# A new order of the work ahead of the attention: softmax before the weight copies, four banks for the values, the norm in two halves of six tiles, and two weight jobs on GpSimd

## What is computed

```python
tokens = conv(x, conv_w, stride 4) + conv_b            # (4, 256, 192)
q, k, v = tokens @ {q,k,v}_w.T + {q,k,v}_b             # 96 wide
img = softmax(q @ k.T / sqrt(96)) @ v @ proj_w.T + proj_b
h = concat(img, txt)                                   # (4, 384, 192)
x_norm = ln(h) ; qkv = x_norm @ Wqkv + bqkv
hidden = silu(x @ Wb1)                                 # x is itself a normed h
h = h + linear_attention(qkv, hidden) @ Wproj + bproj
h = h + experts(ln(h); router_w, w1, w2, top 2 of 8)
```

## Time and profile before

| | |
|---|---|
| runs | 320.44, 320.45, 321.77 us; median 320.45 |
| profiled execution | 316.02 us |
| its span, first to last instruction | 314.3 us |
| busy: PE, DVE, ACT, GpSimd | 76%, 68%, 56%, 37% |
| mean granted clock of PE | 0.872 of 2.4 GHz |
| PE of the chain that ended last | 43% (DVE 24%, ACT 13%, issue 8%, DMA 5%) |

### The profile page before, as it was taken

The page is one execution under the profiler, slowest core; times in us unless marked ns, Lnnn a source line. Parts: engine busy times, 40 slices in busy tenths (PEclk is TensorE's granted clock), DMA queues, the critical chain, the costliest instruction groups (busy, mean ns, idle before and its releaser), DMA issues.

```text
span 314.3 us, 7309 instructions
## 1 busy us (share of the span) xinstructions
PE 239.6 (76%) x2381; PEld 173.0 (55%) x2382; DVE 214.7 (68%) x661; ACT 175.5 (56%) x410; POOL 117.0 (37%) x151
## 2 busy tenths in 40 slices
PE   3876965795767379787969897489999999999400
PEld 3265554353444257466648675357777677777200
DVE  2184986789986648688886799636566566556565
ACT  1347153378788798998891354045655456555100
POOL 5000014154542123223221031455767677773301
PEclk9999977579997597999995589589999999999955
DMA  6991005000000002130001021021122111110085
GB/s 178 313 238 40 3 0 168 34 0 3 1 0 3 0 2 60 45 102 3 4 0 41 0 77 38 25 63 53 62 63 72 45 61 54 41 38 32 7 265 186
DMA packets 13390, 19.01 MB, mean 60 GB/s; under 512 B 3451, under 2 KB 11138, under 8 KB 12850
## 3 DMA queue, kind: packets, MB, share of 16 engines
q1 hardware_dynamic: 10018, 13.90, 14.6%
q0 software_dynamic: 3024, 4.73, 5.1%
q10 hardware_dynamic: 320, 0.01, 0.1%
HBM read 14.69 MB, written 5.41 MB: 64 GB/s over the span
## 4 chain that ended last, share of the span: by engine, by line
PE 43%; DVE 24%; ACT 13%; issue 8%; DMA 5%; SPq 4%; POOL 1%; DVEq 0%; ACTq 0%; POOLq 0%
PE bank L983 4%; PE bank L996 3%; PE bank L998 3%; PE bank L997 3%; DMA qk<-in_w1b 3%; PE bank L900 2%; PE bank L968 2%; DVE third_place L1421 2%; PE bank L972 2%; PE bank L971 2%; PE bank L970 2%; PE bank L969 2%; PE bank L954 2%; DMA v<-y_rows 2%; DVE at_half L1471 2%
## 5 line engine op out<-in xcount | busy, mean ns | idle before, releaser
L1234 ACT ACTIVATE qk<-bank 128x512 f32<-128x512 f32 x31 | 18.5, 597 | 48.6 <-PE bank L972 48.6
L564 POOL DMA_INDIRECT qk<-x_rows,tok_row x32 | 34.7, 1085 | 20.8 <-DVE tok_row L1746 9.4
L569 POOL DMA_INDIRECT y_rows<-qk,dst_row x31 | 31.3, 1010 | 20.6 <-DVE qk L1786 13.7
L996 PE MATMUL bank<-wx,qk 128*128 x124 | 30.5, 246 | 0.7 <-DVE qk L1780 0.5
L997 PE MATMUL bank<-wx,qk 128*128 x124 | 30.5, 246 | 0.0
L998 PE MATMUL bank<-wx,qk 128*128 x124 | 30.5, 246 | 0.0
L1780 DVE COPY qk<-bank 128x512 f16<-128x512 f16 x31 | 13.1, 424 | 24.9 <-PE bank L983 24.3
L1471 DVE SCALAR_TENSOR_TENSOR at_half<-bank,at_half 128x384 f16<-128x384 f32 x48 | 25.1, 549 | 5.0 <-ACT at_half L1149 4.8
L1774 DVE TENSOR_TENSOR qk<-qk 128x512 f16<-128x512 f32 x31 | 21.4, 692 | 10.2 <-ACT qk L1235 10.2
L1149 ACT ACTIVATE at_half<-bank 128x384 f16<-128x384 f32 x48 | 21.3, 511 | 3.6 <-PE bank L800 3.6
L983 PEld LDWEIGHTS bank<-ident,qk 128*128 128x128 f16 x248 | 16.2, 98 | 8.8 <-DVE qk L1774 2.2
(11 more groups left out here) (323 smaller groups left out, 711.2 us busy)
## 6 DMA issues: line engine op xcount, KB each, us to landing
early<-in_w SPq DMA_DIRECT2D x4, 768.0 KB, 4.4
qk<-in_w1a SPq DMA_DIRECT2D x2, 1024.0 KB, 6.0
qk<-in_w1b SPq DMA_DIRECT2D x4, 512.0 KB, 10.3
x_rows<-xr SPq DMA_DIRECT2D x4, 288.0 KB, 2.3
v<-y_rows SPq DMA_DIRECT2D x4, 288.0 KB, 4.9
qk<-y_rows SPq DMA_DIRECT2D x4, 288.0 KB, 5.2
out<-hr SPq DMA_DIRECT2D x4, 288.0 KB, 2.9
at_half<-in_wq SPq DMA_DIRECT2D x1, 704.0 KB
```

The costliest lines, as they stand in the source:

```text
L564: pool.indirect_dma_start(xg[:, i % 4, :], None, x2_dram, bass.IndirectOffsetOnAxis(ap=tok_row[:, i:i + 1], axis=0), bounds_check=NTOK - 1 ...
L569: pool.indirect_dma_start(y_dram, bass.IndirectOffsetOnAxis(ap=dst_row[:, i:i + 1], axis=0), ye[:, i % 4, :], None, bounds_check=2 * NTOK ...
L996: pe.matmul(o_, actT[:, k, 0, c], w[:, W2H + d:W2H + d + D], start=(m == 0), stop=False)
```

## The change

On PE: eight products of a matrix of ones with itself ahead of the first wait; the second half of `g` goes to bank 4; values go to banks 5, 6, 7, 4 and wait for no copy of values; the bias products move ahead of the transpositions of images 0 and 1 (and wait for all four value copies, whose banks they reuse); scores run one step ahead of `himg`; the small products for the output projection move between images 2 and 3; 50 instead of 60 fillers ahead of the slot products, none in place of 20 ahead of the experts.

On ACT: softmax 0 and 1 and the values come before any weight copy; it takes over the copies of the transposed probabilities; weight jobs 0 to 3 are copied behind the values, softmax 2, softmax 3 and image 2. Jobs 0 and 1 are copied with scale 1, since GpSimd scaled them in place.

On GpSimd: it scales jobs 0 and 1 in place when they land, and forms their low halves, job 0's before and job 1's behind the low half of the projection weights, both ahead of `x_low(0)`.

On DVE: no low halves of jobs 0 and 1 and no copies of probabilities; text moments follow the first two maxima; job 2's low half comes behind the maxima of all images, job 3's between `normalize(1)` and `x_t(0)`; the first norm takes six tiles; moments of images 2 and 3 and the second norm (six tiles) are a chain whose steps are put between the instructions of the loop's first rounds (`go_on`), to be finished before tile 6 is normalized.

The counts of `s_w_low` are lowered by two where they are waited for (SP, GpSimd, PE, ACT), and PE and ACT also wait for `s_w_pool_low` at 4. The diff, cut to its core:

```diff
+            def scaled(n):
+
+                w, _high, _low = staged(n)
+                pool.wait_ge(s_w_loaded[n], 16)
+                pool.tensor_scalar(w, w, WS, None, ALU.mult).then_inc(s_w_scaled, 1)
+
+            def pool_low(n):
+
+                pool.wait_ge(s_w_high, n + 1)
+                for half in range(2):
+                    w, high, low = staged(n, half)
+                    pool.tensor_tensor(low, w, high, ALU.subtract).then_inc(s_w_pool_low, 1)
+
+            scaled(0)
+            scaled(1)
+            pool_low(0)
             pool.wait_ge(s_wqhigh_ready, 2)
             pool.tensor_tensor(bias_half[:, 1, :], bq, bias_half[:, 0, :], ALU.subtract).then_inc(s_biaslow_ready, 1)
             pool.tensor_tensor(w_half[:, 1, 0, :], wq[:, 0, :], w_half[:, 0, 0, :], ALU.subtract).then_inc(s_wqlow_ready, 1)
             pool.tensor_tensor(w_half[0:D - P, 1, 1, :], wq[0:D - P, 1, :], w_half[0:D - P, 0, 1, :], ALU.subtract).then_inc(s_wqlow_ready, 1)
 
+
+            pool_low(1)
...
+            pe.wait_ge(s_ones_ready, 1)
+            for _ in range(8):
+                pe.matmul(bank[3][:, 0:P], ones[:], ones[:], start=True, stop=True)
...
-            for i in range(2):
-                if i:
-                    pe.wait_ge(s_g_ready, i)
-                pe.matmul(bank[7][0:NP1, :], mt[:], xp1[:, i * 512:(i + 1) * 512], start=True, stop=True).then_inc(s_g_mm, 1)
+            for i, bk in enumerate((7, 4)):
+                pe.matmul(bank[bk][0:NP1, :], mt[:], xp1[:, i * 512:(i + 1) * 512], start=True, stop=True).then_inc(s_g_mm, 1)
...
-                    pe.wait_ge(s_vp_ready, i - 1)
+                    pe.wait_ge(s_g_ready, i - 1)
...
-                    mm = pe.matmul(bank[5 + i % 2][:, n * D:(n + 1) * D], xp1[:, m0:m0 + P], wv, start=True, stop=True)
+                    mm = pe.matmul(bank[VALUES_AT[i]][:, n * D:(n + 1) * D], xp1[:, m0:m0 + P], wv, start=True, stop=True)
...
-                if b == 0:
-                    pe.wait_ge(s_vp_ready, B)
+                pe.wait_ge(s_vp_ready, b + 1)
...
             scores(0)
             scores(1)
             for i in range(B):
                 values(i)
+            bias_products()
             prob_t(0)
             prob_t(1)
...
-            mm.then_inc(s_mnb_mm, 1)
+            scores(2)
             himg(0)
-            scores(2)
+            scores(3)
             himg(1)
-            scores(3)
             prob_t(2)
+            projection_t()
+            himg(2)
             prob_t(3)
-            himg(2)
+            router_products()
             himg(3)
...
-            keep_busy(60)
+            keep_busy(50)
...
-            keep_busy(20)
...
-                act.activation(high, w, ACT.Copy, scale=WS).then_inc(s_w_high, 1)
+                if n < 2:
+                    act.wait_ge(s_w_scaled, n + 1)
+                else:
+                    act.wait_ge(s_w_loaded[n], 16 * (2 if jobs[n][0] == "w1b" else 1))
+                act.activation(high, w, ACT.Copy, scale=1.0 if n < 2 else WS).then_inc(s_w_high, 1)
 
...
+            def prob_t(b):
+                act.wait_ge(s_pT_mm, b + 1)
+                if b >= 2:
+                    act.wait_ge(s_himg_mm, b - 1)
+                act.activation(probT[:, b % 2, :, :].rearrange("p a n -> p (a n)"), bank[2 + b % 2][:, :], ACT.Copy).then_inc(s_pT_ready, 1)
...
             softmax(0)
+            values(0)
+            values(1)
             softmax(1)
-            weights_high(3)
-            for b in range(B):
-                himg(b)
-                if b + 2 < B:
-                    softmax(b + 2)
-                if b == 1:
-
-                    act.wait_ge(s_wq_ready, 5)
-                    act.activation(w_half[:, 0, :, :], wq, ACT.Copy).then_inc(s_wqhigh_ready, 1)
-                    act.wait_ge(s_bq_ready, 1)
-                    act.activation(bias_half[:, 0, :], bq, ACT.Copy).then_inc(s_wqhigh_ready, 1)
-
+            values(2)
+            values(3)
+            weights_high(0)
+            prob_t(0)
+            prob_t(1)
+            himg(0)
+            softmax(2)
+            weights_high(1)
+            himg(1)
+            softmax(3)
+            weights_high(2)
+            act.wait_ge(s_wq_ready, 5)
+            act.activation(w_half[:, 0, :, :], wq, ACT.Copy).then_inc(s_wqhigh_ready, 1)
+            act.wait_ge(s_bq_ready, 1)
+            act.activation(bias_half[:, 0, :], bq, ACT.Copy).then_inc(s_wqhigh_ready, 1)
+            prob_t(2)
...
+            himg(2)
+            weights_high(3)
+            prob_t(3)
...
+            himg(3)
...
-            weights_low(0)
             negmax(0)
             negmax(1)
+            dve.wait_ge(s_txt_loaded, 16 * B)
+            for b in range(B):
+                moments(b * CT + IT, h[:, b * CT + IT, :])
...
+            row_sums(0)
+            row_sums(1)
             biases()
             negmax(2)
             weight_scales()
             negmax(3)
-            prob_t(2)
-            image_moments(0)
-            image_moments(1)
-            prob_t(3)
-            image_moments(2)
-            two_norms(0, T - CT)
+            row_sums(2)
+            row_sums(3)
+            weights_low(2)
+            finish(image_moments(0))
+            finish(image_moments(1))
+            finish(two_norms(0, 2 * CT))
...
+            def last_rows_norm():
+                yield from image_moments(2)
+                yield from image_moments(3)
+                yield from two_norms(2 * CT, T)
+
             normalize(0)
             normalize(1)
+            weights_low(3)
             x_t(0)
-
-            for n in range(IT):
-                dve.wait_ge(s_himg_ready, (B - 1) * IT + n + 1)
-                moments((B - 1) * CT + n, h[:, (B - 1) * CT + n, :])
-            two_norms(T - CT, T)
+            rows = last_rows_norm()
...
+                if t + 2 == 2 * CT:
+                    finish(rows)
+                go_on(rows)
                 if t + 2 < T:
                     normalize(t + 2)
 
                 dve.wait_ge(s_exp_ready, t + 1)
-                link(dve.tensor_scalar(eb[:, t % 2, :], eb[:, t % 2, :], FS, None, ALU.min))
+                n_min = after(dve.tensor_scalar(eb[:, t % 2, :], eb[:, t % 2, :], FS, None, ALU.min))
+                go_on(rows)
+                dve.wait_ge(s_step, n_min)
...
+                go_on(rows)
...
+                go_on(rows)
+                go_on(rows)
                 if t:
                     queries_low(t - 1)
+                go_on(rows)
+                go_on(rows)
```

More of the change, by code:

```diff
@@ L1317, in weights_low, with moments @@
                     ins.then_inc(s_w_low, 1)
+            def moments(t, src):
+                link(dve.bn_stats(stat[:, t, :], src))
+                link(dve.bn_aggr(mv[:, t, :], stat[:, t, :]))
             def negmax(b):
@@ L1374, in two_norms @@
                 a, r = nwt[:, 0, 0:2 * n], nwt[:, 1, 0:2 * n]
-                link(dve.tensor_scalar(a[:, 0:n], mv[:, t0:t1, 1], EPS, None, ALU.add))
-                link(dve.scalar_tensor_tensor(out=a[:, n:2 * n], in0=a[:, 0:n], scalar=EPS, in1=mv[:, t0:t1, 1], op0=ALU.mult, op1=ALU.add))
-                for _ in rsqrt_steps(r, a, 2 * n):
-                    pass
+                k = after(dve.tensor_scalar(a[:, 0:n], mv[:, t0:t1, 1], EPS, None, ALU.add))
+                yield
+                dve.wait_ge(s_step, k)
+                k = after(dve.scalar_tensor_tensor(out=a[:, n:2 * n], in0=a[:, 0:n], scalar=EPS, in1=mv[:, t0:t1, 1], op0=ALU.mult, op1=ALU.add))
+                yield
+                dve.wait_ge(s_step, k)
+                yield from rsqrt_steps(r, a, 2 * n)
                 dve.tensor_copy(r12[:, t0:t1], r[:, n:2 * n])
@@ L1392, in prob_t @@
-                dve.tensor_copy(probT[:, b % 2, :, :].rearrange("p a n -> p (a n)"), bank[2 + b % 2][:, :]).then_inc(s_pT_ready, 1)
             def image_moments(b):
-                for n in range(IT):
-                    dve.wait_ge(s_himg_ready, b * IT + n + 1)
-                    moments(b * CT + n, h[:, b * CT + n, :])
-            dve.wait_ge(s_txt_loaded, 16 * B)
-            for b in range(B):
-                moments(b * CT + IT, h[:, b * CT + IT, :])
-            weights_low(1)
-            weights_low(2, (0,))
@@ L1404, in _ @@
-            prob_t(0)
-            prob_t(1)
-            weights_low(2, (1,))
-            weights_low(3)
+                for t in range(b * CT, b * CT + IT):
+                    dve.wait_ge(s_himg_ready, b * IT + t % CT + 1)
+                    k = after(dve.bn_stats(stat[:, t, :], h[:, t, :]))
+                    yield
+                    dve.wait_ge(s_step, k)
+                    k = after(dve.bn_aggr(mv[:, t, :], stat[:, t, :]))
+                    yield
+                    dve.wait_ge(s_step, k)
@@ L1408, in _, with go_on, finish, together @@
+            def go_on(chain):
+                next(chain, None)
+            def finish(chain):
+                for _ in chain:
+                    pass
```

(13 more changed lines are left out.)

101 lines of the change are left out of this document (49 added, 52 removed).

## The result

The changed kernel takes 321.23 us (median of 20 runs, 319.62 to 327.35), the kernel before 320.24 on the same chip (20 runs, 316.55 to 322.37). The ratio counts only executions within 1.5% of the fastest of their kernel (12 of the 20 before, 19 of the 20 after), and by it the changed kernel takes 1.0128 of the time before, with an interval of 1.0103 to 1.0153. The size is less sure than that interval looks: the means of the executions counted, 318.65 and 321.27 us, differ by 0.8%, and the medians of all 20 by 1.0 us, 0.3%. So it is **slower, by 0.3 to 1.3%**, 1 to 4 us; measured again (last but one of the experiments) it was 1.019 by the ratio and 1.3% by the medians. The profiled execution took 320.58 us around a span of 318.8, against 316.02 and 314.3.

The account below looks back on a forecast made before the run. It took chains of waits over the first 75 us and the seam before the expert loop as the bound; +1.9 at tile 5 and -1.0 at the seam gave +0.9, so 321.3 us, range 315.0 to 325.0.

Parts of the forecast that it names:

- Set-up, "I take 0" for the clock: PE's start: whether eight products of ones raise the clock, 0 to -1.9 us on set-up products; 0 taken.
- Bias products, 28.9: PE's bias products ahead of the transposes: start 24.0, last 4.9 us, end 28.9 (-6.4); wholly at 1.2 GHz, 30.2.
- Copy 2 ends at 39.3, the high halves at 41.2: ACT's weight copy 2, then projection weights' and bias's high halves: done at 41.2 instead of 45.6, -4.4 us.
- N: Start of the first normalized tile on DVE, ahead of the expert loop: 53.2 us, forecast not to move.
- rival B: PE stays at 1.2 GHz through bias products and transposes; DVE 1.3 to 3 us later: 322.6 to 324.5; chance 0.25.
- A: The forecast itself: -1.5 to +2.5 us as the clock at set-up and the seam fall, 319.0 to 323.0; chance 0.42.
- Each step lets one whole GpSimd instruction pass: DVE's six-tile norm beside GpSimd's queue: four instructions end during it, the fourth at 50.3; thirteen steps left, 2.8 us.
- Rival C: Small norm steps slip past GpSimd; first normalized tile at 48 to 51, total 315.0 us; chance 0.20.
- After N: First loop rounds: tile 0 2 us later, tile 1 -0.5, moments and norm steps in gaps; +1.9 at tile 5.
- Seam, -1.0: Before the expert loop, without 20 fillers: transposes start earlier, first expert products at low clock; 0 to -3, taken -1.0 us.
- Rival E: Nothing moves: bias products' wait for parameters eats ACT's reordering, gathers bind the seam; 320.5 us; chance 0.08.
- Rival D: Eight products of ones bring 2.4 GHz for all set-up, score and value products: 311.4 us; chance 0.05.

Follow-up runs that it names:

- last but one of the experiments: The changed kernel run again, unedited, beside the kernel before: ratio 1.019 (1.013 to 1.025), profiled span 318.8 us.

## Why the prediction was right and wrong

- **Set-up, "I take 0" for the clock:** -1.2 to -1.8 us at `mt` in five of nine executions, about 0 in four; inside the bounds, and the value taken is right for the rest. That the small products "never raised" the clock was right too: in the changed kernel they ran on from 9 to 21 us at 1.2 GHz, after it had been up.
- **Bias products, 28.9:** 28.78, by two errors that cancel: 6.7 us long and not 4.9 (1.2 GHz throughout, which I had put at 6.2), started at 22.1 and not 24.0. In the late set-ups with GpSimd's scaling, where they don't cancel, it was 31.5 to 32.0.
- **GpSimd's scaling, 2.0 with an upper bound of 4.0:** 5.38 and 5.36 us, above the bound. One operand isn't half the price of two: two operands of 1024 columns take 2.10 us here (4.20 for two), one operand of 2048 takes 5.4. The Trainium skill, "GPSIMD Engine Reference", section "Engine selection", calls one-input work roughly line-rate, which gave an estimate of about 1.7 us; the trace disagrees by a factor of three. Off the path with the early set-up; with the late one it holds the second softmax for 4 us.
- **"Copy 2 ends at 39.3, the high halves at 41.2":** the step that failed. ACT ended copy 2 at 42.2 and the bias's high half at 44.0, as softmax 2 waited for the image products at 1.2 GHz (L673, 2.93 us) and softmax 3 stood behind a weight copy and the second image's. PE's scores of image 2 (2.07 us) and first image products (2.93) took 2.3 us longer than the same rows at 2.4 GHz before (1.13 and 1.57). So GpSimd's queue ended at 52.9 and not 50.3: 2.6 of the 2.8 us by which N was missed. This is rival B in the form of its upper end ("when the image products are slow too"), with the bias products' own lateness hidden by the early set-up; the forecast took A. B's upper end should read 324.3, 321.3 + 3, and not 324.5. Putting the projection weights first in ACT's order (with VectorE's norm ahead of the weights) took it away.
- **"Each step lets one whole GpSimd instruction pass":** wrong; the first step let all of them pass, 5.96 us in place of four steps of 1.5 to 2. That left 17 steps, 3.1 us, and not 13 and 2.8: 0.3 us. That the halves on GpSimd would be paid in N was right, and its price, 4.2 us, is measured by moving them. Rival C (the steps slip past) falls by the same row.
- **After N:** +2 at tile 0 (1.85 measured, beyond N's shift), -0.5 at tile 1 (-0.3), +1.9 at tile 5 (+2.0). The terms hold.
- **Seam, -1.0:** -0.5, within its range; in the kernel before the edit alone gives -0.45. Between tile 5 and the indices another 0.3 us came in, which I had not counted.
- **Rival E** (nothing moves) falls with the milestones: -6.6 us at the bias products, +4.9 in the loop. **Rival D** falls: the clock did rise in the set-up, and the dense 49-row work that followed ran at 1.2 GHz.
- **The lock.** The Trainium skill, "SBUF — State Buffer", section "Who interferes with whom", has the two engines share one pair of ports as an exclusive lock, which a one-input instruction outside the two-port modes doesn't need. The trace agrees in this: the moments (`BATCH_NORM_STATS2`) kept their 0.36 us at 44.5 to 46.7 under GpSimd's subtractions. The kernel before had shown it too, though I said that no row tests it: its moments took 0.36 us at 48.02 and 48.63, under a running GpSimd subtraction. By the page a blocked instruction waits for the other's "whole instruction"; here it waited for the rest of one and three more in a row.

With N 2.8 too early, the seam 0.5 too good and 0.3 uncounted, the sum is +4.5 instead of +0.9. For the profiled pair the forecast of no change that can be measured is wrong by that; my chance of slower was 0.35. That the medians moved by 1.0 us, as forecast, doesn't bear the terms out.

## What to carry to other kernels

Before work is moved from VectorE to GpSimd, ask what VectorE wants to do while GpSimd's queue runs: here a full queue held even a step of 0.2 us to its end, and moving the queue only moves the hold, unless it falls where VectorE is idle or does moments. When an early stage gains much, follow the gain to the next engine's order of work; here it ended behind two weight copies on ScalarE, and with the urgent copy ahead of them GpSimd started at 39.20 instead of 44.09. A median that agrees with a forecast says nothing of its terms; the milestones do.

## What was not expected of the hardware

- VectorE's instruction wasn't let in between GpSimd instructions queued back to back: it took 5.96 us under the rest of one and three more, 1.80 under the rest of one and one more, 7.21 for a pair of its own; a pause of 0.92 us of GpSimd was enough to let it in. It works both ways: 2.28 us for a GpSimd instruction of 0.42 beside two of VectorE. It isn't always so: in the earlier trace rows the two took turns, and what makes the difference was not tested.
- GpSimd scales 128x2048 float32 in place in 5.4 us, 2.6 ns per column, more than its subtraction of two operands costs per column (2.05 ns).
- The same set-up code, run behind the same eight products, had the higher clock in five profiled executions and not in four.
